# Two layers of attention on one core: the first norm's row sums from a second load of the input, and a ScalarE cast moved

## The reference, cut to what matters

```python
B, T, D, H, HID = 16, 256, 256, 16, 1024          # one x of (16, 256, 256), f32
def norm(x, t, gw, gb, bw, bb):                    # the input's norm is the first use of it
    return (t @ gw.T + gb) * x * rsqrt(mean(x * x, -1) + 1e-6) + (t @ bw.T + bb)
# layer 0
x1 = x + attention(norm(x, cond, g1...), Wq, Wk, Wv, Wo)
x2 = x1 + silu(n @ gate.T) * (n @ hid.T) @ out.T,  n = norm(x1, cond, g2...)
# and x = x + x2 of layer 0
# layer 1: masked attention with its own weights, an rms norm and a modulation of its output
y = x + modulate(rmsnorm(attention(x, mask)))
```

## Time and profile before

| | |
|---|---|
| median of 3 runs | 1013.13 us (1011.05 to 1015.7) |
| the profiled execution | 1008.46 us, its span 1006.6 us |
| granted TensorE clock, mean | 0.967 |
| PE busy | 909.2 us (90%) |
| PE weight loads | 780.6 us |
| DVE, ACT, POOL busy | 570.3, 547.5, 415.2 us |
| DMA | 91.29 MB, 91 GB/s in the mean |
| DMA share by slices | 0.2 to 0.3 in layer 0, 0.6 to 0.7 in layer 1 |

### The profile page before, as it was taken

How to read it: one execution, slowest core, us unless ns; L and a number is a source line. 1 busy time by engine, 2 the same in 40 slices (tenths; PEclk the granted TensorE clock), 3 DMA queues, 4 the chain that set the end, 5 groups by cost and what they waited for, 6 DMA issues and landing times.

```text
span 1006.6 us, 24326 instructions
## 1 busy us (share of the span) xinstructions
PE 909.2 (90%) x8188; PEld 780.6 (78%) x8188; DVE 570.3 (57%) x1104; ACT 547.5 (54%) x1130; POOL 415.2 (41%) x633
## 2 busy tenths in 40 slices
PE   3578899999999999999999999999999789888874
PEld 3456698898888988988889889889887677777653
DVE  3366556557555565575565756545455455555541
ACT  2246556546455565464554665554556566666652
POOL 5223344443443444434334344344444454444522
PEclk9779999999999999999999999999999999999997
DMA  6555423322332233223322242232437576576611
GB/s 204 110 106 122 91 64 75 75 65 59 66 86 42 63 73 73 63 58 68 84 42 63 69 91 65 65 76 66 94 74 167 119 160 147 142 166 144 157 36 34
DMA packets 83070, 91.29 MB, mean 91 GB/s; under 512 B 7776, under 2 KB 70016, under 8 KB 83008
## 3 DMA queue, kind: packets, MB, share of 16 engines
q1 hardware_dynamic: 83008, 90.50, 39.8%
HBM read 60.30 MB, written 29.36 MB: 89 GB/s over the span
## 4 chain that ended last, share of the span: by engine, by line
PE 73%; issue 8%; DVE 7%; ACT 5%; POOL 3%; DMA 1%; SPq 1%; POOLq 0%; DVEq 0%; ACTq 0%
PE work L525 11%; PE work L527 11%; PE work L526 11%; PE pvps L622 8%; PE s2ps L606 7%; PE s1ps L583 5%; PE work L710 4%; PE acc L525 3%; PE acc L526 2%; PE acc L527 2%; PE work L656 2%; PE s1ps L568 2%; PE work L718 1%; DVE rest L919 1%; DVE th L959 1%
## 5 line engine op out<-in xcount | busy, mean ns | idle before, releaser
L1055 ACT ACTIVATE E<-s2ps 128x512 f32<-128x512 f32 x384 | 214.1, 596 | 184.2 <-PE s2ps L606 110.8
L882 DVE TENSOR_REDUCE nmax<-s1ps 128x2 f32<-128x512 f32 x256 | 163.9, 682 | 32.1 <-PE s1ps L583 31.9
L525 PE MATMUL work<-xch,Gh 128*128 128x256 f32 x512 | 154.5, 302 | 0.0
L959 DVE SCALAR_TENSOR_TENSOR th<-th,work 128x256 f32<-128x256 f32 x128 | 53.8, 420 | 168.7 <-ACT th L1073 168.7
L1328 POOL TENSOR_TENSOR hl<-hf,hh 128x256 fp32r<-128x256 f32 x128 | 94.9, 742 | 131.0 <-PE acc L527 77.3
L526 PE MATMUL work<-xcl,Gh 128*128 128x256 f32 x512 | 147.1, 287 | 0.0
L527 PE MATMUL work<-xch,Gl 128*128 128x256 f32 x512 | 146.9, 287 | 0.0
L606 PE MATMUL s2ps<-stack 100*128 100x256 bf16 x768 | 127.7, 275 | 2.1 <-DMA stack<-rows 2.0
L875 DVE TENSOR_REDUCE nmax<-s1ps 128x4 f32<-128x512 f32 x128 | 85.6, 685 | 36.5 <-PE s1ps L568 36.4
L525 PEld LDWEIGHTS work<-xch,Gh 128*128 128x128 f32 x512 | 99.3, 194 | 8.2 <-issue 6.6
L622 PE MATMUL pvps<-E,vaug 128*32 128x256 f32 x1536 | 97.5, 387 | 6.3 <-ACT E L1055 4.0
(11 more groups left out here) (131 smaller groups left out, 2149.1 us busy)
## 6 DMA issues: line engine op xcount, KB each, us to landing
stack<-scr SPq DMA_DIRECT2D x64, 384.0 KB, 4.6
stack<-scr SPq DMA_DIRECT2D x64, 256.0 KB, 5.2
scr<-qp SPq DMA_DIRECT2D x64, 192.0 KB, 2.3
scr<-kp SPq DMA_DIRECT2D x64, 192.0 KB, 2.3
stack<-scr SPq DMA_DIRECT2D x64, 128.0 KB, 5.6
X<-xT SPq DMA_DIRECT2D x16, 256.0 KB, 4.5
yT<-crm SPq DMA_DIRECT2D x16, 256.0 KB, 5.2
stack<-rows SPq DMA_DIRECT2D x196, 4.0 KB
```

Of the source, the lines that this page charges most:

```text
L525: mm(out, lh, rh, start=first, stop=False, skip_group_check=True)
L882: v.tensor_reduce(nmax[:, g // 4, qh, 2 * (g % 4):2 * (g % 4) + 2], s1ps[u % 2][:, :].rearrange("p (h t) -> p h t", h=2), AX_X, ALU.max, n ...
L959: v.scalar_tensor_tensor(th[:, i % 2, :], th[:, i % 2, :], 1.0, bank[:, 0:T], ALU.add, ALU.mult).then_inc(silu_ready, 1)
L1055: a.activation(E[:, exp_slot(st.L["B2"], st.full, g, kh), :], s2ps[g % 2 if short else u % 2][:, :], ACT.Exp, scale=SCORE_SCALE).then_inc( ...
```

## The change

The input is given to the program a second time as `x_rows`, with rows (tokens) on the partitions. SP loads 256 KB of it per sample into `dg`. ACT squares it in place, DVE sums along the free dimension and adds epsilon, POOL takes the root. SP writes the 256 roots to a scratch in HBM and reads them back to all partitions into `crm`'s first half. DVE multiplies X by them in slot 5, and ACT's block for N moves from the end of slot 7 to the end of slot 6. The squares on POOL, the N part of `mean_squares`, of the diagonals and of the spreading matmul go. On ACT, where the key is of layer 1, the cast of its middle part moves from the end of slot 1 to slot 2, behind `oh` and the exponentials.

```diff
 def ms_slot(L):
-    if L["N"] == 0 or L["C"] == 0:
-        return 5
-    return None if L["C"] is None else 6
+    return None if L["C"] is None else 5 + L["C"]
...
-        if g == 6:
-            uses += ["bcC"] * (L["C"] == 0) + ["bcN"] * (L["N"] == 0)
+        if g == 6 and L["C"] == 0:
+            uses.append("bcC")
...
+            def load_rows(n):
+                sp.dma_start(flat(dg[:, :, :]), x_rows[:, bass.ds(n * TC * D, TC * D)]).then_inc(rows_loaded, 16)
+
+            load_rows(0)
             load_x(0)
...
+                def roots_out():
+                    if L["N"] == 0:
+                        after(sp, n_rstd, roots_made)
+                        sp.dma_start(r_scr, rstd[:, 0:2]).then_inc(n_written, 16)
+
+                def roots_in():
+                    if L["N"] == 0:
+                        after(sp, n_written, roots_written)
+                        if st.s0 == FIRST:
+                            sp.wait_ge(cond_mm, 1)
+                        if L["C"] is not None:
+                            after(sp, c_lo, gains_split)
+                        sp.dma_start(spread,
+                                     bass.AP(r_scr.tensor, 0, [[0, P], [1, T]])).then_inc(n_spread, 16)
...
                     write_parts(par, 0, qp, q_written)
+                    roots_out()
                     after(sp, k_low, a_split)
                     write_parts(par, 3 * DH, kp, k_written)
                     after(sp, q_written, a_written)
                     after(sp, k_written, a_written)
+                    roots_in()
...
+                if L["N"] == 0:
+                    after(sp, sums_ready, summed)
+                    if gain_spread is not None:
+                        after(sp, *gain_spread)
+                    load_rows(st.n(4))
...
+            def row_sums(st):
+                n = st.n(3)
+                after(dve, sq_n, n + 1)
+                v.tensor_reduce(sums[:, :], flat(dg[:, :, :]).rearrange("p (t d) -> p t d", t=TC), AX_X, ALU.add)\
+                 .then_inc(sums_ready, 1)
+                after(dve, sums_ready, n + 1)
+                v.tensor_scalar(var[:, 0:2], sums[:, :], EPS, VAR_TOP, ALU.add, ALU.min).then_inc(n_var, 1)
+
+            def normalize_n(st):
+                after(dve, x_loaded, 16 * (st.n(3) + 1))
+                after(dve, n_lo, st.n(3))
+                after(dve, n_spread, 16 * (st.n(3) + 1))
+                by_row = spread.rearrange("q (p c) -> q c p", c=TC)
+                v.tensor_tensor(nrm[:, :, :].rearrange("p c (t q) -> p c t q", t=TC),
+                                X[:, bass.ds(st.n(3), 1), :, :].rearrange("p o c (t q) -> p (o c) t q", t=TC),
+                                by_row[:, None, :, :].to_broadcast([P, FC, TC, P]), ALU.mult).then_inc(n_normed, 1)
...
+                    if g == 1 and L["N"] == 0:
+                        row_sums(st)
                     if L["C2"] is not None:
                         swiglu(st, g)
+                    if g == 5 and L["N"] == 0:
+                        normalize_n(st)
...
             def step(st):
                 L = st.L
-                if st.s0 == FIRST:
-                    act.wait_ge(cond_ready, 2)
...
+                    if g == 2 and L["A"] == 1:
+                        middle(st, "K", kp, k_mid)
                     if g == 2 and L["R"] is not None:
...
-                    if g == 7 and L["N"] == 0:
+                    if g == 0 and L["N"] == 0:
                         n = st.n(3)
-                        b, k = st.bank("bcN")
-                        after(act, work_free[b], k + 1)
+                        after(act, rows_loaded, 16 * (n + 1))
+                        a.activation(flat(dg[:, :, :]), flat(dg[:, :, :]), ACT.Square, scale=D ** -0.5).then_inc(sq_n, 1)
+                    if g == 6 and L["N"] == 0:
+                        n = st.n(3)
+                        if st.s0 == FIRST:
+                            act.wait_ge(cond_ready, 2)
+                        after(act, n_normed, n + 1)
                         affine(st, nrm, C_G1, C_B1, n, n_affine, 2 * (n + 1))
                         a.copy(xnh[1 - st.par][:, :, :], nrm[:, :, :]).then_inc(n_hi, 1)
...
-                    if g == q_slot(L, 1):
+                    if g == 2 and L["A"] == 0:
                         middle(st, "K", kp, k_mid)
...
-                    if g == 2:
-                        if L["N"] == 0:
-                            n = st.n(3)
-                            after(pool, x_loaded, 16 * (n + 1))
-                            after(pool, n_lo, n)
-                            p.tensor_tensor(nrm[:, :, :], xb(n), xb(n), ALU.mult).then_inc(sq_n, 1)
+                    if g == 1 and L["N"] == 0:
+                        after(pool, n_var, st.n(3) + 1)
+                        p.tensor_tensor(rstd[:, 0:2], var[:, 0:2], power[:, 0:2], ALU.pow).then_inc(n_rstd, 1)
```

More of the change, by code:

```diff
@@ L283, in build @@
         rstd = sb("rstd", [P, 4], F32)
+        sums = sb("sums", [P, TC], F32)
+        spread = crm[:, 0, :]
         nmax = sb("nmax", [P, 2, TC, 8], F32)
@@ L451, in step @@
                 x_before = held(16 * n_x)
+                summed = held(n_x + 1)
+                roots_made, roots_written = held(n_x + 1), held(16 * (n_x + 1))
+                gains_split = held(st.n(-1))
+                gain_spread = None
+                if L["C"] == 0:
+                    b, k = st.bank("bcC")
+                    gain_spread = (work_full[b], held(k + 1))
                 scratch_read = held(48 * (n_a - 1))
@@ L699, in mean_squares, with broadcast_rstd @@
                 bank, full = open_bank(st, "ms")
[L700 to L709, removed]
-                            last = mm(bank[:, col + t:col + t + 1], src[:, c, P * t:P * (t + 1)],
-                                      mean1[:, :], start=c == 0, stop=c == FC - 1, skip_group_check=True)
+                after(pe, sq_c, st.n(-1) + 1)
+                src = dg[:, :, :].rearrange("p (c u) t -> p c (u t)", c=FC)
+                for t in range(TC):
+                    for c in range(FC):
+                        last = mm(bank[:, t:t + 1], src[:, c, P * t:P * (t + 1)],
+                                  mean1[:, :], start=c == 0, stop=c == FC - 1, skip_group_check=True)
                 last.then_inc(full, 1)
-            def broadcast_rstd(st, use, col):
+            def broadcast_rstd(st, use):
                 bank, full = open_bank(st, use)
-                after(pe, diag_ready, st.n(2 if use == "bcR" else 3) + 1)
-                mm(bank[:, 0:T], ones[:, :], dg[:, col:col + 2, :].rearrange("p a b -> p (a b)"),
+                after(pe, diag_ready, st.n(-2 if use == "bcR" else -1) + 1)
+                mm(bank[:, 0:T], ones[:, :], dg[:, 2:4, :].rearrange("p a b -> p (a b)"),
                    start=True, stop=True).then_inc(full, 1)
@@ L802, in step @@
                         swiglu_down(st.n(-3), HC - 2 + g)
-                    if g == 6:
-                        if L["C"] == 0:
-                            broadcast_rstd(st, "bcC", 2)
-                        if L["N"] == 0:
-                            broadcast_rstd(st, "bcN", 0)
+                    if g == 6 and L["C"] == 0:
+                        broadcast_rstd(st, "bcC")
             def short():
@@ L1289, in step @@
                         after(pool, work_free[b], k + 1)
-                        b, k = st.bank("bcR") if L["R"] is not None else \
-                            st.last().bank("bcN" if st.last().L["N"] == 0 else "bcC")
-                        after(pool, work_full[b], k + 1)
+                        if L["R"] is not None or st.last().L["C"] == 0:
+                            b, k = st.bank("bcR") if L["R"] is not None else st.last().bank("bcC")
+                            after(pool, work_full[b], k + 1)
+                        if L["N"] == 0:
+                            after(pool, sums_ready, st.n(3) + 1)
+                        elif st.last().L["N"] == 0:
+                            pool.wait_ge(rows_loaded, 16 * (B + 1))
                         p.tensor_tensor(dg[:, :, :].rearrange("p (c u) t -> p c (u t)", c=FC),
```

46 lines of the change are left out of this document (21 added, 25 removed).

## The result

The changed kernel takes 1049.44 us in the median of 4 runs (1046.9 to 1050.69), the kernel before 1013.45 in its runs beside it: a ratio of 1.0352, with a 95% interval of 1.0321 to 1.0383. The forecast was 1008.1, between 997 and 1017.

A forecast was written before the change was run, and what follows sets the result against it. PE was taken to bound layer 0 (busy 39.05 of 39.60 us), with its largest layer 1 wait for `ol`. Terms -6.8 + 0.4 + 5.2 + 7.6 - 11.4 = -5.0 us, from 1013.13 to 1008.1, range 997 to 1017.

The forecast's parts named there:

- (a): Layer 0: PE no longer does N's mean squares (0.90 us) and spreading matmul (0.77 us), together 1.67 us a step.
- (b): Layer 0: ACT's earlier N block delays the values, overhang 0.28 us; a step gains 0.62, eleven steps -6.8 us.
- (c): Steady step's other additions on ACT, DVE, POOL and SP cost 0; steps 0 and 1 add 0.4 us.
- (d): Start: row load, root write and spread delay the first projection to near 31.1 us; +5.2 us, between +2.5 and +7.
- lower case, +2.9: Start: if the root write does not queue behind the 1 MB load, it lands near 19.8 and the sum is +2.9.
- The spread lands 2.3 later: Start: the spread lands 2.3 us behind the root write's landing near 22.2, so near 24.8.
- (e): Steps 14 to 17: the later key cast makes PE wait 2.2 us in two steps, 1.6 in two: +7.6 us.
- (f): Steps 19 to 29, layer 1: `oh` 1.04 us earlier shortens the wait for `ol`; eleven steps, -11.4 us.
- It holds by 0.5 us: Layer 1: half 0's read lands at 867.3, ahead of the next step's first scores at 867.8.
- R2: Layer 1: half 0's read lands 1.0 us later, cancelling the gain at `ol`; sum +6.4, 1019.5 us; chance 0.13.
- R1: Layer 0: PE's saving comes in full, up to 1.67 us a step, 18.4 in eleven: 996.5 us; chance 0.12.
- R4: No stall in steps 14 to 17, or the start queues less; sum -12.6, 1000.5 us; chance 0.18.

The follow-up runs named there:

- x8: Changed kernel with the key's cast back in its old place and, in steps up to 0, the spread issued right behind the key's write: 1006.69 us, ratio 0.9934.
- x13: Changed kernel with the key's cast in its old place and the spread reading 128 KB of row input, 1 KB per partition: 1004.35 us, ratio 0.9906.
- x9: x8 with VectorE's multiply and ScalarE's block behind it at the end of slot 7 in steps -2 to 0: 1008.42 us, ratio 0.9946.
- x2: Kernel before with the key's middle cast moved into slot 2, behind the exponentials, in steps 14 to 17 alone: 1022.95 us, ratio 1.011.
- x6: x3 with SP issuing the row reads ahead of the store of y: 1010.65 us, ratio 0.9984 of the kernel before.
- x14: Changed kernel with SP issuing the row reads ahead of the store of y: 1027.69 us, ratio 1.0139 of the kernel before.
- x3: Kernel before with the key's middle cast moved into slot 2, behind the exponentials, from step 18 on alone: 1033.74 us, ratio 1.0199.
- x12: x8 with C's mean squares issued twice in steps 1 to 12, sixteen narrow matmuls in a row: 1019.72 us, ratio 1.0067.

## Why the prediction was wrong

**(a) and (b), layer 0: right in kind, short in size.** Forecast -0.62 a step, measured -0.76 (38.84 for 39.60), with the wait of 0.73 ahead of the values where it was named. VectorE's new operation took 0.81 in the median and 0.82 at most, against 0.69 in the start, so the 0.13 taken for it was right. A full wait for an `hl` did not come, and could not: in each step of this stretch the `hl` beside it has at most 0.27 us left when the multiplication starts. What the sum lacked is the clock: five steps of the kernel before took 1.5 us more than the 39.60 of the earlier trace rows, and none of the changed kernel's did. That is another -7.5, and -15.8 in all. The forecast read one smooth step and multiplied it.

**(c), the additions of a steady step at nothing: right** in layer 0, where the steps come out at the forecast's length although the spread lands 2 us later than assumed.

**(d), the start: the term of the sum that was mis-sized, +24.5 for +5.2.** Two steps of it failed. (Its lower case, +2.9, does not follow from its rows either: a write that lands 2.4 sooner makes +2.3 of the 4.7.) "The spread lands 2.3 later", taken from the key write's row of like size, was 4.9 (issued at 21.85, landed by 26.8). The root write was right: forecast 22.2, its successor issued at 21.85. That accounts for step -3, where the first projection came at 33.37 and not near 31. And only step -3 was worked through. For the steps behind it the forecast used the steady step's reading, that the spread "is ready about 10 us before slot 5". In steps of 24 to 27 us it was the last thing to come, with waits of 11.1, 5.5 and 6.1 us. x8 shows 4.7 us of the start's loss to be SP's order and x13 shows 7.0 to be the spread's source; x9 shows that VectorE's order is none of it. The rest, 12.8 us if these two add up (no run has both), was not taken apart; the two transfers in a row of step -3 are in it, and the bytes of the row loads may be.

**(e): right.** Four waits of 7.2 us in all for a forecast of 7.6, in the changed kernel and in x2 alike. The stretch grew by 10.2, as the clock fell too (0.98).

**(f), the same in layer 1: the step that turned the sign, +21.6 for -11.4.** Its gain came: the wait for `ol` fell from 15.9 to 5.4 us. Its price was worked out right too: half 0's read was issued 5.66 us behind the start of `oh`, where 4.16 + 0.5 + 1.04 = 5.70 was forecast. What failed is "It holds by 0.5 us", and for two reasons.

First, the margin was read from step 24, and that is the one step of 18 to 28 in the kernel before in which the clock had fallen. It fell right behind the wait for `ol`, ahead of the scores whose start the slack was measured to. Step 23 and step 24 of the kernel before:

```profile
838.86:856.21 17.35, 15.48 (x154) 12.43 (x154) 9.90 (x20) 11.57 (x23) 8.36 (x14) 1.00 0.69 153
856.21:874.79 18.58, 16.79 (x154) 13.94 (x154) 9.86 (x20) 11.46 (x24) 8.38 (x14) 0.91 0.62 142
```

In the step ahead of it the read is issued at 842.99 and the first scores that need it start at 850.18:

```profile
842.99 1.26 SPq L422 DMA_DIRECT2D stack<-scr  x3
```

```profile
850.18 0.40 PE L568 MATMUL s1ps<-stack 97*128 97x128 bf16 x4
```

Its last transfer goes out near 843.8 and lands at 849.4 by the earlier trace rows. That is 0.76 us of slack, and a shift of 1.04 + 0.5 makes it -0.78. The wait measured in step 23 is 0.82. The forecast's own arithmetic on the neighbouring step would have given the wait that came.

Second, it counted the read of half 0 and not what is queued behind it. TensorE needs the rows right after the first scores. They stand in SP's queue behind half 0 and the result's store, and their wait (16.7 us in this stretch) is the larger one. x6 and x14 show it by what one exchange of two issues gives back (23.1 us against x3, 21.8 against the changed kernel). The Trainium skill ("DMA: Bandwidth & Descriptors", section "Queues, rings and completion order") says that each DMA engine takes its descriptors in the order of the ring, and that an increment lands only after the engine's earlier writes. By it 12 KB issued behind 1 MB are as late as the 1 MB. x6 agrees: with 256 KB less ahead of them the wait for the rows fell from 14.5 to 2.9 us.

The waits alone cost 11 us more than in the kernel before. The lower clock made nearly 22 of it, and the forecast had no term for it.

**The rivals.** R2 had the place, the read into the stack in layer 1, and the side. Its price was too low: it let the new wait cancel the old one and did not see that behind the two waits for the stack the clock also falls to half. R1's 18 us in layer 0 came out at 15.8, but by the clock and not by the second part of PE's saving. R4 is excluded by x2.

## What to carry to other kernels

When one wait is shortened, work out the slack of the next bound from several steps, and first look whether the step it is read from has the mean clock and length of its neighbours. Follow the queue past the transfer in question to the last small one that the same engine's next instruction needs, and put small urgent transfers ahead of large patient ones. A part that is hidden in the steady step must be costed again for the short steps at the start, where the same transfers have less time.

## What the hardware showed that was not expected

- TensorE's clock fell to 0.5 for about 3 us behind a run of sixteen matmuls with one column each, without any idle time (five of eleven steps of the kernel before, 1.5 us each, and three of eleven in x12); it never fell behind the runs of eight in steps 2 to 12 of the changed kernel and x8. What decides in which steps it falls stays open.
- It also fell behind two waits of 0.8 and 1.2 us that stood close together (eight of the changed kernel's steps 18 to 28 have the lower clock), and mostly not behind the single wait of 1.6 us of the kernel before. The one time in steps 18 to 28 that it fell there, a step of 17.4 us took 18.6.
- A transfer of one kilobyte to each of 128 partitions landed in 4.4 us when all read the same kilobyte of the scratch, and in 2.1 when each read its own kilobyte of the input. Reads queued behind the first landed 0.4 to 0.9 us later.
- The write of 256 roots, 1 KB in pieces of 8 bytes, took 3.6 to 3.9 us to land in the median, longer than the key write of 192 KB (2.3).
